# Order of the instructions and waits in the leaf sweeps of a tridiagonal eigensolver

## What is computed

```python
def _L0_gnn_ref(features, A, W1, b1, W2, b2):
    deg = jnp.sum(A, axis=0) + jnp.sum(A, axis=1) - jnp.diagonal(A)
    d_inv_sqrt = jnp.where(deg > 0, jax.lax.rsqrt(deg), 0.0)
    L = jnp.diag(deg) - A
    L_norm = d_inv_sqrt[:, None] * L * d_inv_sqrt[None, :]
    _, U = jnp.linalg.eigh(L_norm)
    agg = jnp.einsum('mn,bnd->bmd', U.T, features)
    h = jax.nn.relu(agg @ W1 + b1)
    out = h @ W2 + b2
    return jnp.einsum('nm,bmd->bnd', U, out)
...
x = _layernorm(x + _L0_gnn_ref(...), axis=-1)
# then layers 1 (LSTM over windows), 2 (batch norms) and 3 (attention), each with residual and layer norm
```

## Time and profile before

| | |
|---|---|
| median of 3 runs | 2143.85 us (2143.3 to 2145.32) |
| the profiled execution | 2142.91 us, span 2141.1 us |
| PE busy | 1787.1 us, 83% of the span |
| DVE busy | 1441.6 us, 67% |
| ACT busy | 857.2 us, 40% |
| POOL busy | 661.5 us, 31% |
| sweeps | from about 225.6 to 442.7 us |

### The profile page before, as it was taken

The page is one execution under the profiler, slowest core; times in us unless marked ns, Lnnn a source line. Parts: engine busy times, 40 slices in busy tenths (PEclk is TensorE's granted clock), DMA queues, the critical chain, the costliest instruction groups (busy, mean ns, idle before and its releaser), DMA issues.

```text
span 2141.1 us, 32310 instructions
## 1 busy us (share of the span) xinstructions
PE 1787.1 (83%) x9764; PEld 1536.2 (72%) x9764; DVE 1441.6 (67%) x5778; ACT 857.2 (40%) x1766; POOL 661.5 (31%) x1058
## 2 busy tenths in 40 slices
PE   3455333324999999999999999999999999989998
PEld 2333333313999788888889999988888888768886
DVE  7999999986777556544444444444444677877886
ACT  2333122211443466333333333323323465756664
POOL 0011344412234367432333323333332111651221
PEclk9999766656999999999999999999999999999999
DMA  6000000000111000000000000000010311320111
GB/s 192 2 1 2 1 1 1 1 1 20 60 40 40 30 15 15 15 5 10 10 11 10 10 0 10 20 1 0 0 39 10 148 60 60 101 69 21 40 41 60
DMA packets 44705, 62.72 MB, mean 29 GB/s; under 512 B 13985, under 2 KB 33313, under 8 KB 44449
## 3 DMA queue, kind: packets, MB, share of 16 engines
q1 hardware_dynamic: 43984, 61.08, 8.4%
q10 hardware_dynamic: 592, 0.17, 0.0%
HBM read 36.08 MB, written 25.17 MB: 29 GB/s over the span
## 4 chain that ended last, share of the span: by engine, by line
PE 67%; DVE 5%; ACT 3%; POOL 1%; issue 1%; ACTq 0%; another core or an unknown queue 0%; DVEq 0%; POOLq 0%
PE ps L2164 43%; PE ps L2553 4%; PE ps L2755 2%; PE ps L1688 2%; PE ps L1713 2%; PE ps L2769 2%; PE ps L1674 1%; PE ps L1698 1%; PE ps L2809 1%; PE ps L2803 1%; ACT l_raw L1585 1%; PE ps L1665 1%; DVE j_lnstats L1571 1%; PE ps L2792 1%; DVE x L1562 1%
## 5 line engine op out<-in xcount | busy, mean ns | idle before, releaser
L2295 ACT ACTIVATE l_gates<-ps,biases 128x512 f32<-128x512 f32 (+1 forms) x504 | 289.3, 636 | 490.3 <-remote 475.8
L2164 PE MATMUL ps<-l_nodes_in,l_even 128*128 128x512 f32 x1392 | 321.3, 390 | 2.6 <-DVE x L1562 1.9
L2164 PEld LDWEIGHTS ps<-l_nodes_in,l_even 128*128 128x128 f32 x1392 | 260.7, 188 | 59.2 <-DVE x L1562 2.7
L2164 PE MATMUL ps<-l_nodes_in,kept 128*128 128x336 f32 (+1 forms) x1280 | 298.0, 350 | 2.0 <-ACT l_gates L2295 1.8
L2396 DVE TENSOR_TENSOR l_gates<-l_gates 128x512 f32<-128x512 f32 (+1 forms) x72 | 50.3, 698 | 343.1 <-ACT l_gates L2295 343.1
L2076 POOL CAST l_nodes_in<-big 128x512 fp32r (+3 forms) x142 | 100.5, 737 | 549.3 <-remote 519.6
L2164 PEld LDWEIGHTS ps<-l_nodes_in,kept 128*128 128x128 f32 x1280 | 229.2, 188 | 27.4 <-issue 4.3
L2164 PE MATMUL ps<-l_state,l_even 128*128 128x512 f32 x960 | 223.3, 392 | 0.0
L2164 PEld LDWEIGHTS ps<-l_state,l_even 128*128 128x128 f32 x960 | 180.3, 188 | 39.8
L2079 POOL TENSOR_TENSOR l_nodes_in<-big,l_nodes_in 128x512 fp32r<-128x512 f32 (+1 forms) x142 | 200.5, 1433 | 5.7
L995 PE MATMUL ps<-w,sw_xT 128*128 128x128 f32 x256 | 58.2, 419 | 133.8 <-ACT sw_xT L859 133.8
(11 more groups left out here) (581 smaller groups left out, 3889.2 us busy)
## 6 DMA issues: line engine op xcount, KB each, us to landing
x<-in_x SPq DMA_DIRECT2D x4, 2048.0 KB, 16.9
residual<-s_x SPq DMA_DIRECT2D x16, 512.0 KB, 2.6
x<-residual SPq DMA_DIRECT2D x16, 512.0 KB, 5.3
normed<-l_raw SPq DMA_DIRECT2D x16, 512.0 KB, 2.6
x<-normed SPq DMA_DIRECT2D x16, 512.0 KB, 3.2
out<-a_y SPq DMA_DIRECT2D x15, 512.0 KB, 2.9
l_raw<-in_L_gnn_W SPq DMA_DIRECT2D x16, 256.0 KB, 2.7
l_raw<-in_L_gnn_W SPq DMA_DIRECT2D x4, 512.0 KB, 3.6
```

The lines of the kernel that those rows point to most:

```text
L2164: return pe.matmul(ps[:, 4 * j + gate, 0:n], weight[w_part][:, at:at + 128].bitcast(F32R), src[:, part, k, 0:n].bitcast(F32R), start=start ...
L2295: act.activation(gates[:, j, gate, 0:n], ps[:, 4 * j + gate, 0:n], ACT.Tanh if gate == G else ACT.Sigmoid, bias=bias[:, gate * KD + j:gate ...
```

## The change

- The sweep no longer begins with dd, H and thr. They stand at the end of the sweep before, interleaved with down and ee: up, d, down, dd, ee, thr, H. For the first sweep `begin` computes them. The last sweep computes them for a sweep that doesn't follow.
- ns comes ahead of H2, and pre ahead of s4. The sum of neighbours goes from between the scans to behind node, and now waits for hs.
- mx goes from between d and ee to behind node and the sum in the next sweep (`if before`); after the last sweep `turn_z` computes it.
- floor waits for eb_ready, N2 no longer; rn waits for dm_ready of its own sweep in place of sq_ready of the sweep before.
- Waits dropped since another, later one implies them: sum_ready at nv, neb_ready at C1a, tst_ready at nm, sgs_ready at CS, sg_ready at xx, ppx at GX. hsR no longer waits for hs, since the sum has done so.
- On ACT the root R comes ahead of the sine roots. dm adds the constant 1.0 in place of the tile of ones.

The diff, cut to its core:

```diff
@@ begin()
+                stt(E["dd"], d[:, 0:n1], EPS * EPS, d[:, 1:L], ALU.mult, ALU.mult).then_inc(c, done.one())
+                tt(SH[1][:, 2, :], d[:, 0:n1], d[:, 1:L], ALU.subtract).then_inc(c, mark("H"))
+                dve.wait_ge(c, done.n)
+                stt(E["thr"], E["dd"], -1.0, E["dd"], ALU.mult, ALU.max).then_inc(c, mark("thr"))
@@ sweep(), first part
-                after("d")
-                stt(E["dd"], ...
-                after("d")
-                tt(SH[turn % 2][:, 2, :], ...
-                after("dd")
-                stt(E["thr"], ...
+                after("thr", "ee")
+                tt(E["ns"], E["thr"], E["ee"], ALU.is_lt).then_inc(chain[0], mark("ns"))
                 after("H")
                 tt(E["H2"], ...
-                after("thr", "ee")
-                tt(E["ns"], ...
...
-                after("d")
-                tt(SH[turn % 2][:, 1, :], d[:, 0:n1], d[:, 1:L], ALU.add).then_inc(sum_ready, 1)
...
+                after("hs")
+                tt(SH[turn % 2][:, 1, :], d[:, 0:n1], d[:, 1:L], ALU.add).then_inc(sum_ready, 1)
+                if before:
+                    reach(cs2_ready, before)
+                    tt(mx[:, :, :], cs2[:, :, :], floor[:, :, :], ALU.max).then_inc(mx_ready, 1)
                 reach(r_ready, turn)
-                after("hs")
                 tt(E["hsR"], ...
...
-                reach(sum_ready, turn)
                 after("hsR")
                 stt(E["nv"], ...
...
-                    reach(sq_ready, before)
+                    reach(dm_ready, turn)
                     dve.reciprocal(rn[:, :, :], sq[:, :, :]).then_inc(rn_ready, 1)
...
-                reach(neb_ready, turn)
                 after("al")
                 tt(C1[:, 0, :, BASE:BASE + L], ...
...
-                reach(tst_ready, turn)
-                    reach(sgs_ready, before)
...
-                reach(act_ready, turn)
+                reach(eb_ready, turn)
                 ts(floor[:, 0, :], ...
...
-                reach(eb_ready, turn)
                 after("p2")
                 scan(V["N2"], ...
...
-                reach(sg_ready, turn)
...
-                after("ppx")
@@ sweep(), end
+                after("x1", "G")
+                tt(d, V["G"], V["x1"], ALU.subtract).then_inc(chain[0], mark("d"))
                 ...
                 tt(E["down"], ...
-                after("x1", "G")
-                tt(d, ...
-                reach(cs2_ready, turn)
-                after("floor")
-                tt(mx[:, :, :], ...
+                after("d")
+                stt(E["dd"], ...
                 after("up", "down")
                 tt(E["ee"], ...
+                after("dd")
+                stt(E["thr"], ...
+                after("d")
+                tt(SH[following % 2][:, 2, :], ...
@@ turn_z()
+                reach(cs2_ready, turn)
+                tt(mx[:, :, :], cs2[:, :, :], floor[:, :, :], ALU.max).then_inc(mx_ready, 1)
@@ ACT, sweep()
+                act.wait_ge(s4_ready, turn)
+                act.activation(E["R"], E["s4"], ACT.Sqrt).then_inc(r_ready, 1)
                 if before:
                     sine_roots(before)
-                act.wait_ge(s4_ready, turn)
-                act.activation(E["R"], E["s4"], ACT.Sqrt).then_inc(r_ready, 1)
                 act.wait_ge(dm1_ready, turn)
-                act.activation(V["dm"], V["dm1"], ACT.Identity, bias=t["ones"][0:N, 0:1], scale=1.0).then_inc(dm_ready, 1)
+                act.activation(V["dm"], V["dm1"], ACT.Identity, bias=1.0, scale=1.0).then_inc(dm_ready, 1)
```

More of the change, by code:

```diff
@@ L610, in begin, with sweep @@
                 ts(E["es"], E["xx"], -1.0, None, ALU.add).then_inc(c, mark("es"))
+                stt(E["dd"], d[:, 0:n1], EPS * EPS, d[:, 1:L], ALU.mult, ALU.mult).then_inc(c, done.one())
+                tt(SH[1][:, 2, :], d[:, 0:n1], d[:, 1:L], ALU.subtract).then_inc(c, mark("H"))
+                dve.wait_ge(c, done.n)
+                stt(E["thr"], E["dd"], -1.0, E["dd"], ALU.mult, ALU.max).then_inc(c, mark("thr"))
                 count["d"] = count["z"] = count["sha"] = done.n
-            def sweep(turn, before, last=None):
-                after("d")
-                stt(E["dd"], d[:, 0:n1], EPS * EPS, d[:, 1:L], ALU.mult, ALU.mult).then_inc(chain[0], mark("dd"))
-                after("d")
-                tt(SH[turn % 2][:, 2, :], d[:, 0:n1], d[:, 1:L], ALU.subtract).then_inc(chain[0], mark("H"))
-                after("dd")
-                stt(E["thr"], E["dd"], -1.0, E["dd"], ALU.mult, ALU.max).then_inc(chain[0], mark("thr"))
+            def sweep(turn, before, following, last=None):
+                after("thr", "ee")
+                tt(E["ns"], E["thr"], E["ee"], ALU.is_lt).then_inc(chain[0], mark("ns"))
                 after("H")
                 tt(E["H2"], SH[turn % 2][:, 2, :], SH[turn % 2][:, 2, :], ALU.mult).then_inc(chain[0], mark("H2"))
-                after("thr", "ee")
-                tt(E["ns"], E["thr"], E["ee"], ALU.is_lt).then_inc(chain[0], mark("ns"))
-                after("H2", "ee")
-                stt(E["s4"], E["ee"], 4.0, E["H2"], ALU.mult, ALU.add).then_inc(s4_ready, 1)
                 after("ns")
@@ L631, in sweep @@
                      mark("pre"))
-                after("d")
-                tt(SH[turn % 2][:, 1, :], d[:, 0:n1], d[:, 1:L], ALU.add).then_inc(sum_ready, 1)
+                after("H2", "ee")
+                stt(E["s4"], E["ee"], 4.0, E["H2"], ALU.mult, ALU.add).then_inc(s4_ready, 1)
                 after("pre")
@@ L636, in sweep @@
                      ALU.mult).then_inc(act_ready, 1)
+                after("H")
+                ts(E["hs"], SH[turn % 2][:, 2, :], 0.0, 0.5, ALU.is_ge, ALU.subtract).then_inc(chain[0], mark("hs"))
+                reach(act_ready, turn)
+                tt(V["node"], actp[:, 1:L + 1], actp[:, 0:L], ALU.max).then_inc(chain[0], mark("node"))
                 if last:
@@ L640, in sweep @@
                         *((active_ready, 1) if last == "signal" else (chain[0], mark("active"))))
-                after("H")
-                ts(E["hs"], SH[turn % 2][:, 2, :], 0.0, 0.5, ALU.is_ge, ALU.subtract).then_inc(chain[0], mark("hs"))
-                reach(act_ready, turn)
-                tt(V["node"], actp[:, 1:L + 1], actp[:, 0:L], ALU.max).then_inc(chain[0], mark("node"))
+                after("hs")
[3 more added lines that the diff above has]
+                    tt(mx[:, :, :], cs2[:, :, :], floor[:, :, :], ALU.max).then_inc(mx_ready, 1)
                 reach(r_ready, turn)
-                after("hs")
                 tt(E["hsR"], E["hs"], E["R"], ALU.mult).then_inc(chain[0], mark("hsR"))
@@ L753, in sweep @@
                 tt(E["down"], E["eY"], V["rY"][:, 1:L], ALU.mult).then_inc(chain[0], mark("down"))
[L754 to L758 removed]
+                after("d")
+                stt(E["dd"], d[:, 0:n1], EPS * EPS, d[:, 1:L], ALU.mult, ALU.mult).then_inc(chain[0], mark("dd"))
                 after("up", "down")
                 tt(E["ee"], E["down"], E["up"], ALU.mult).then_inc(chain[0], mark("ee"))
+                after("dd")
+                stt(E["thr"], E["dd"], -1.0, E["dd"], ALU.mult, ALU.max).then_inc(chain[0], mark("thr"))
+                after("d")
+                tt(SH[following % 2][:, 2, :], d[:, 0:n1], d[:, 1:L], ALU.subtract).then_inc(chain[0], mark("H"))
             def turn_z(turn):
+                reach(cs2_ready, turn)
+                tt(mx[:, :, :], cs2[:, :, :], floor[:, :, :], ALU.max).then_inc(mx_ready, 1)
                 reach(sq_ready, turn)
@@ L812, in _ @@
                     next_chain(chains[i // SPAN])
-                sweep(i + 1, i, "signal" if i + 1 == FIRST_SWEEPS else None)
+                sweep(i + 1, i, i + 2, "signal" if i + 1 == FIRST_SWEEPS else None)
             turn_z(FIRST_SWEEPS)
@@ L825, in _ @@
                     with dve.Fori(0, more):
-                        sweep(1, 0, "count")
+                        sweep(1, 0, 1, "count")
                         turn_z(1)
```

3 lines of the change are left out of this document (removed).

## The result

| | before | changed |
|---|---|---|
| median | 2143.82 us (4 runs) | 2131.47 us (4 runs, 2131.13 to 2133.11) |
| ratio | | 0.9942, 95% interval 0.9928 to 0.9957 |
| the profiled execution, span | 2142.91, 2141.1 us | 2133.11, 2131.1 us |
| the 31 periods of the sweeps, first x1 to last | 210.51 us | 200.74 us |

The change makes the kernel 12.4 us faster (9.2 to 15.4 by the interval). The prediction said 2141.2 us and at least 2134.5, so it was wrong, and on the good side. Against the 3.1 us forecast for the sweeps the profiled pair shows 9.8.

A forecast was written before the change was run, and what follows sets the result against it. VectorE's serial sweeps were taken to bound the kernel: gross .26 us a sweep less .16 of POOL collisions, net .10, times 31 is 3.1, less .5 once, from 2143.85 to 2141.2 us. Range 2134.5 to 2143.8; high-end gain bound 2133.5.

The forecast's parts named there:

- Where it matters: The 32 sweeps, where VectorE is nearly always busy: a microsecond off them is a microsecond off the time.
- The doubled waits: At nv, C1a and N2: a late supplier's wait doubled with another, long satisfied one costs .06 to .07 us.
- x1 to nv: Turn of the sweep: 2.09 us becomes 1.99, a gain of .10, less a .02 hold on sum.
- C1a: L672 without neb_ready starts .06 to .07 earlier, falls .05 behind POOL's L900, is held, and keeps .01 us.
- dm: ACT activation ahead of rn: taken at .21 us, no stall, .06 cover; if still .31, rn stalls .04 to .05.
- The tail: Once, after the last sweep: x1 to mx grows by .4 us; a wait at the start adds .1.
- ppn's hold: After N2 and pp: ppn meets POOL's L919 and is held some .08 us, leaving .01 of a .09 gain.
- POOL's L902 and C1 then meet as they do now: Behind C1a: the meeting of C1 (L677) with POOL's L902, which held C1 for .09 us, stays unchanged.
- The hold on sum: In the turn of the sweep: sum starts .05 behind a POOL instruction and is held .02 us.
- Rival 1: POOL isn't met: if ppn or C1a slips by, .18 to .35 us a sweep, 2133.5 to 2138.8 us; chance .36.
- rival 2: The waits are free and merely re-ordering gives nothing: 2144.3 us; chance .08.
- rival 3: POOL holds C1a, ppn and sum for its whole length: net loss .30 us a sweep, 2153.7 us; chance .06.

The follow-up runs named there:

- e4: Changed kernel with a second, long satisfied wait added ahead of C3, T4 and P: 2139.93 us, ratio .9996.
- e2: Kernel before with every wait kept, but the late supplier's wait written first at nv, C1a and N2: 2133.75 us, ratio .9965.
- e6: Changed kernel with al's second wait, for dm, written out again ahead of its wait for nsig: 2133.36 us, ratio .9961.
- e5: Changed kernel with dm's bias taken from the tile of ones again, dm .31 us long for .22: 2133.40 us, ratio .9958.
- e3: Changed kernel with the second waits back at nv (sum_ready), C1a (neb_ready) and N2 (eb_ready): 2138.86 us, ratio .9987.
- e1: Kernel before, order and bias kept, with only the waits dropped that the change drops: 2136.05 us, ratio .9972.
- e11: Changed kernel with one more satisfied wait ahead of POOL's product w, so that w starts later: 2134.81 us, ratio .9961.
- e8: Changed kernel with POOL's sum SA moved from the sweep's end to behind ad1 of the next, beside reciprocal rn: 2131.17 us, ratio .9946.
- second profile: Profile of the changed kernel, unaltered, run again on another chip: 2131.41 us, ratio .9955.
- e7: Changed kernel with ndx and floor changing places, so ndx no longer meets POOL's CZ: 2132.72 us, ratio .9951.

## Why the prediction was wrong, step by step

**Right.** *Where it matters:* the rest behind the sweeps is 1699.0 and 1698.9 us, so the gain of the profiled pair is that of the sweeps. That the two are so near is in part chance: between 500 and 520 us the changed kernel's profile loses 2.3 us to the other, near 1815 and 1915 us it wins back 2.9. *The doubled waits:* the three places and their price (.06 to .07) were right; e4 measures .070. The reason given, that the wait is doubled, was half of it: e2 shows that the late one must be the one that stands alone. *x1 to nv:* forecast net 2.01, measured 1.982. *C1a:* gain and hold cancel but for .01 (al to C1 .486 to .476 in the median), forecast .01. The offset behind w was wrong even so: forecast .05, measured .006, and C1a was held until .104 behind w's start, forecast .11. al had two waits too, and as rn now waits for dm, al's own wait for it falls away; e6 puts it back and has the offset at .044. *dm:* .216 for the .21 assumed; e5 gives the stall of .046 without it. *The tail:* the last x1 to layer 0's first product is .4 us longer (62.8 before, 442.1 to 504.85; 63.2 after, 432.3 to 495.5), as forecast; the .1 at the start didn't show.

**Wrong.** Forecast .10 net a sweep, measured .259 in the median and .315 in the mean. The steps that failed are, above all, two meetings with POOL: ppn's, priced at .08, which cost nothing, and C1's, taken as unchanged, which gave .044.

1. *ppn's hold, .08.* It didn't occur. This was a tie read as a defeat: ".51 to .52 behind L716, and POOL's L919 .51 behind it". In the trace ppn starts .000 to .003 ahead of q1 in all 31 sweeps and lasts .159, as in the first sweep, where q1 isn't run. No run shows the .08. Since p2 to x1 gained .087 for the forecast .01, this is .077.
2. *"POOL's L902 and C1 then meet as they do now."* They met .012 apart before (ta first, C1 held .094 in each sweep). In the first profile of the changed kernel they start within .004 of each other in 17 sweeps, in the 14 others C1 is .12 ahead, and it isn't held in any. C1 to C2 gained .044: half of the hold, as nm behind C1 is now held .06 by the same ta.
3. *x1 to nv* gained .109 and not .08: .03. Most of it is x1 to d, .26 for the .28 forecast: x1 was taken as held by POOL, .25 long, and lasts .16, while up behind it is held. The hold on sum, .02 in the forecast, was .034: in 30 sweeps sum (L643) starts .046 to .050 behind POOL's ad1 and lasts .190 to .193, in the two others .155 and .158.
4. *The sweeps that are longer than the median.* In the kernel before the 31 periods sum to 1.8 us more than 31 times their median; in the changed one the two agree. Of the 1.8, 1.1 are six single gaps of .11 to .28 in six different places that have no place in the pattern, such as the one ahead of L723 here:

```profile
345.82 0.18 DVE L721 TENSOR_TENSOR_SCAN sw_buf<-sw_buf,sw_squares 64x16 f32<-64x16 f32 x1
346.21 0.17 DVE L723 TENSOR_TENSOR sw_buf<-sw_Pp 64x16 f32<-64x16 f32 x1 [0.20 <-issue]
```

The changed kernel has none in either profile, nor has any of its variants that adds no wait on DVE; e6, with 31 instructions more on the page, has one, e3 and e4, with 96 more, have three each, e1 has one, e2 four. They go with the number of separate waits; why, no run here tells. The rest does belong to the pattern: seven times, where the chain semaphore is changed, a sweep is .11 longer, and the last one's extra reduction costs .20. The changed kernel pays .09 and .08 for these, .7 us in all, and agrees with its median only because 14 of its sweeps are short ones in which C1a escapes. The prediction looked for none of this. Item 4 is .056 a sweep, of which the gaps are .035.
5. *The clock, 2 us.* The profiled pair is 10.0 us apart in span, the medians 12.4; in the later comparisons the kernel before had medians of 2142.0 to 2142.4 instead of 2143.8. The clock of .66 in 520 to 525 us is 1.7 us short of the full clock (.34 of 5 us, an estimate), and the range had no room for as much.

Items 1 to 3 make .15 of the .159 between .10 and .259; item 4 is the rest to .315.

**Rival 1 was the case.** Its condition was that ppn or C1a slips by: ppn did in every sweep, C1a in 14 of 31, and C1, which the condition didn't name, in all. Its price, .18 to .35 a sweep, holds the .315 measured; its 2133.5 us doesn't reach the 2131.47, for want of the clock's 2 us. It had .36 of the chance. What spoke against it, "L677 and L723 show holds at exactly such offsets", was the weak step: L677 had been .012 behind POOL and L723 .04, and a timeline of two digits can't tell .003 ahead from .010 behind. What spoke for it, that a start .01 ahead of POOL's isn't held, shows in the kernel before at up (L750), .005 to .008 ahead of z in 28 sweeps and .156 long in the median, and at G (L746), .007 to .009 ahead of SA in 29 and .156 long; ndx, .002 to .005 ahead of CZ in the changed kernel, is .054 longer. With three ties of this kind the forecast should have been that some go one way and some the other, and the range should have run down to the stated bound of 2133.5 less the 1.7 of the clock (item 5); that is 2131.8, and still .3 above the result (2131.47).

**Rivals 2 and 3 fall.** e4 prices the wait that rival 2 held free, at .069 to .070. And 253 instructions are gone with the change, each a wait that stood alone (L578, 255 before and two after); e6 agrees: 31 second waits, 31 instructions. As to rival 3: no hold here lasts as long as POOL's instruction; C1a's ends .104 behind the start of w, which lasts .242 (last section). The ties agree with theory F of e11, that who starts first goes first, to a few ns of the recorded starts, and no better: ndx starts .002 to .005 ahead of POOL's CZ and is longer by .054 in every sweep in which CZ is run.

## What to carry to other kernels

In a chain of short VectorE instructions look for suppliers followed by a gap of .10 where others have .03, and write the late supplier's wait first or drop the other: here .07 each time (.22 a sweep for the three in e2), with no other edit. Where two engines' instructions start within .01 of each other in the timeline, treat who is held as unknown, cost the change both ways, and if the finer starts are to be had read them; moving POOL's instruction can decide it: by one wait (C1a .184 for .281 in e11) or beside the reciprocal (up .180 for .247 in e8). And judge a change of 1 to 3 us by its own stretch of the trace: here the work behind the sweeps took 5.5 us more in e11 than in the changed kernel's second profile, while the sweeps differed by 1.1. Before such a difference is put down to an edit, compare two profiles of the same kernel: the changed kernel's own two differ by 2.4 us there.

## What the runs showed of the hardware

- *A hold ends long before POOL's instruction does.* Offset plus hold, in the changed kernel, for POOL instructions of different lengths: SA (.296 long) .077 + .091 = .168, shm (.324) .127 + .069 = .196, z (.233) .076 + .023 = .099, w (.242) .006 + .098 = .104. Each is POOL's length less .12 to .14. In the kernel before: ta (.242) .012 + .093 = .105, q (.207) .046 + .023 = .069, SA (.295) .077 + .090 = .167, z (.230) .076 + .024 = .100. CZ (.243) is the exception: ndx starts .003 ahead of it, and is longer by only .054. VectorE goes on while POOL's record still runs for that long; whether POOL is through with the operands by then or its record is too long, no run tells.
- *The tie.* In the changed kernel's first profile C1a starts .005 to .008 behind w. At .005, in 14 sweeps, it lasts .183 and w .302; at .006 and more, in 17, it lasts .28 and w .242. In its second profile C1a escapes in 3 sweeps, and of the three at .005 one escapes and two are held, so the border isn't sharp in the record. In the first profile the sweeps in which it escapes last 6.38 to 6.43, the others 6.48 to 6.56. A nanosecond or two in the record go with .05 to .1 us, and no edit is needed to change sides.
- *A hold isn't always a loss.* In e6 a delay of .038 ahead of a held instruction cost nothing; in e7 the removal of a hold of .054, with an instruction moved for it, gave .017; in e11 a later POOL made VectorE faster.
- *A wait can lengthen the instruction instead of delaying it.* al, with two waits, lasts .164, and .125 with one (L666 in e6 and in the changed kernel's timeline, .13), at the same start, .25 behind that of the accumulator read in both.
